# A gated cross-attention block with experts: the attention's gate and sum, and the experts' shares, change places

## The reference

```python
x = x + tanh(g_xattn) * xattn(layernorm(x), ctx, ctx)       # 16 heads of 16, softmax over 512 keys
x = x + tanh(g_ffn) * ffn(layernorm(x))

def xattn(q, k, v):                       # per head
    return softmax(q @ k.T * 16 ** -0.5) @ v

def ffn(x):
    h = x + attention(rmsnorm(x, g1), wq, wk, wv, wo)       # causal, rotary, 16 heads
    return h + moe(rmsnorm(h, g2))

def moe(x):                               # 8 experts, 2 per row
    probs = softmax(x @ w_router)
    topw, topi = top_k(probs, 2); topw = topw / sum(topw)
    return sum_k topw[k] * ((silu(x @ wg[e_k]) * (x @ wu[e_k])) @ wd[e_k])
```

## Time and profile before

| | us |
|---|---|
| median of 3 runs | 1544.46 |
| the runs | 1543.71 to 1545.99 |
| the profiled execution | 1545.92 |
| its span, first to last instruction | 1544.1 |
| TensorE busy | 1426.3 (92%) |
| VectorE busy | 1006.0 (65%) |
| ScalarE busy | 779.5 (50%) |
| GpSimd busy | 881.0 (57%) |
| granted TensorE clock, mean | 0.984 |

### The profile page before, as it was taken

How to read it: one execution, slowest core, us unless ns; L and a number is a source line. 1 busy time by engine, 2 the same in 40 slices (tenths; PEclk the granted TensorE clock), 3 DMA queues, 4 the chain that set the end, 5 groups by cost and what they waited for, 6 DMA issues and landing times.

```text
span 1544.1 us, 30418 instructions
## 1 busy us (share of the span) xinstructions
PE 1426.3 (92%) x9013; PEld 856.7 (55%) x9013; DVE 1006.0 (65%) x2351; ACT 779.5 (50%) x1783; POOL 881.0 (57%) x1147
## 2 busy tenths in 40 slices
PE   3999999999999998999999998878899999999997
PEld 1332334444444444444444545457788888888886
DVE  5888767757766765865864755626665656656564
ACT  1576665665665674565666555543233333333332
POOL 7585776974976977787779687445321222222222
PEclk9899999999999998999999999999999999999999
DMA  7756365474574564555473545383354355255220
GB/s 200 193 169 182 97 204 177 147 221 127 176 218 149 169 198 158 174 171 189 141 219 110 175 145 172 130 308 95 64 150 115 79 150 154 43 150 152 39 41 11
DMA packets 116514, 230.12 MB, mean 149 GB/s; under 512 B 20101, under 2 KB 82949, under 8 KB 114310
## 3 DMA queue, kind: packets, MB, share of 16 engines
q1 hardware_dynamic: 81394, 150.29, 31.9%
q0 software_dynamic: 26032, 69.82, 16.5%
q10 hardware_dynamic: 8932, 8.07, 2.0%
HBM read 135.10 MB, written 93.14 MB: 148 GB/s over the span
## 4 chain that ended last, share of the span: by engine, by line
PE 70%; DVE 9%; POOL 9%; issue 5%; ACT 3%; DMA 2%; SPq 1%; another core or an unknown queue 0%; POOLq 0%; DVEq 0%; ACTq 0%
PE pv_ps L1124 10%; PE max_ps L1086 9%; PE max_ps L779 9%; PE key_ps L779 9%; PE key_ps L1103 8%; PE pv_ps L813 6%; DVE neg L1409 4%; PE aux L1172 3%; PE aux L1163 3%; PE pv_ps L815 3%; PE turn_ps L800 2%; PE aux L1156 2%; ACT probs L1295 2%; POOL w_parts L1751 1%; PE key_ps L1106 1%
## 5 line engine op out<-in xcount | busy, mean ns | idle before, releaser
L1409 DVE TENSOR_REDUCE neg<-max_ps 128x1 f32<-128x512 f32 (+3 forms) x864 | 542.3, 665 | 275.3 <-PE max_ps L1089 173.4
L1295 ACT ACTIVATE probs<-key_ps 128x512 f32<-128x512 f32 (+3 forms) x1024 | 499.3, 519 | 370.2 <-PE key_ps L1106 172.5
L1086 PE MATMUL max_ps<-k_stack,q_stack 96*128 96x512 bf16 (+3 forms) x1024 | 354.7, 350 | 32.8 <-DVE neg L1409 18.8
L1103 PE MATMUL key_ps<-q_stack,k_stack 99*128 99x512 bf16 (+3 forms) x1024 | 349.9, 343 | 21.9 <-ACT probs L1295 14.3
L612 POOL DMA_INDIRECT out<-part,whose x71 | 109.8, 1546 | 349.6 <-DVE part L664 277.0
L1086 PEld LDWEIGHTS max_ps<-k_stack,q_stack 96*128 96x128 bf16 x1024 | 100.8, 99 | 222.3 <-DVE neg L1409 124.7
L1103 PEld LDWEIGHTS key_ps<-q_stack,k_stack 99*128 99x128 bf16 x1024 | 100.6, 98 | 120.5 <-ACT probs L1295 56.6
L813 PE MATMUL pv_ps<-weights,hidden_t 128*128 (+1 forms) x426 | 160.0, 413 | 1.4 <-DVE hidden_t L689 1.4
L779 PE MATMUL max_ps<-weights,rows_t 128*128 (+2 forms) x642 | 154.1, 385 | 0.0
L779 PE MATMUL key_ps<-weights,rows_t 128*128 (+2 forms) x636 | 151.1, 382 | 1.1 <-issue 1.1
L1124 PE MATMUL pv_ps<-probs,v_cross 128*32 128x512 f32 (+3 forms) x1024 | 132.1, 587 | 3.4 <-ACT out_t L1365 2.1
(11 more groups left out here) (240 smaller groups left out, 2237.4 us busy)
## 6 DMA issues: line engine op xcount, KB each, us to landing
w_split<-w_parts POOLq DMA_DIRECT2D x32, 704.0 KB, 5.4
weights<-w_split SPq DMA_DIRECT2D x8, 2816.0 KB
weights<-w_split SPq DMA_DIRECT2D x8, 1280.0 KB
w_split<-w_parts POOLq DMA_DIRECT2D x16, 512.0 KB, 4.1
kept_sb<-kept SPq DMA_DIRECT2D x16, 512.0 KB
rows<-rows_in ACTq DMA_DIRECT2D x61, 129.0 KB
parts_cross_k<-parts_k SPq DMA_DIRECT2D x48, 128.0 KB
parts_cross_q<-parts_q SPq DMA_DIRECT2D x48, 128.0 KB
```

Source lines behind the costliest of these rows:

```text
L1086: r = mm(ps[:, 0:keys], q_stack[g][0:KROWS, hd, qt * P:(qt + 1) * P], k_stack[g][0:KROWS, hd, 0:keys], start=True, stop=not own)
L1103: r = mm(ps[:, q0:S], k_stack[g][0:KROWS + NEGROWS, hd, kt * P:(kt + 1) * P], q_stack[g][0:KROWS + NEGROWS, hd, q0:S], start=True, stop=no ...
L1295: act.activation(probs[:, kt % 2, hd, q0:S], key_ps[j % 2][:, q0:S], ACT.Exp).then_inc(m["exp_done"], 1)
L1409: v.tensor_reduce(neg[:, g % 2, hd - place_:hd + 1, qt], scores, op=ALU.max, axis=AX.X, negate=True).then_inc(m["max_red"], many)
```

## The change

The gate tanh(g_xattn) is multiplied into the values (not into their column of ones), so that the attention comes out gated. The sum of x1 is then a plain add; for batches 2 to 6 GpSimd makes it, first thing in stage 7 of step b - 2, and VectorE only waits for each half before its bn_stats. The first half's unit on VectorE moves from 118 to 122 (and its bn_stats from 119 to 123). For batches 0 to 5 GpSimd makes the shares too, in stage 7 of step b + 1, behind the x1 sum; the reciprocal is a power of -1 there. `values(0)` needs the gate and goes behind `x_rows(1)`.

```diff
-X1_SUMS = {b: at(b - 2, 118, 128) for b in BATCHES} | {0: at(-1, 112, 114), 1: at(0, 46, 48), LAST: at(LAST - 2, 112, 114)}
+X1_SUMS = {b: at(b - 2, 122, 128) for b in BATCHES} | {0: at(-1, 112, 114), 1: at(0, 46, 48), LAST: at(LAST - 2, 112, 114)}
...
+X1_SUM_STAGE = {b: stage(b - 2, 7) for b in range(2, LAST)}
+ROUTE_STAGE = {b: stage(b + 1, 7) for b in range(LAST - 1)}
...
                         act.wait_ge(m["gap_r"], b + 1)
+                        over(act, m["route"], b)
                         act.activation(e_gap[:, :], gap[:, :], ACT.Exp).then_inc(m["gap_exp"], 1)
...
-                v.memset(half[:, :], -0.5)
+                v.memset(half[:, 0:QT], -0.5)
+                v.memset(half[:, QT:2 * QT], -1.0)
...
-                        chain.link(v.tensor_copy(pos_i[:, b % 2, :], pos_f[:, :]))
-                    if c == 2:
+                        v.tensor_copy(pos_i[:, b % 2, :], pos_f[:, :]).then_inc(m["placed"], 1)
+                        dve.wait_ge(m["placed"], b + 1)
+                    if c == 2 and b not in ROUTE_STAGE:
+                        dve.wait_ge(m["route"], b)
                         dve.wait_ge(m["gap_exp"], b + 1)
...
-                        if b == LAST - 2:
-                            put_in_order()
+                    if c == 2 and b == LAST - 2:
+                        dve.wait_ge(m["gap_exp"], b + 1)
+                        put_in_order()
...
-                            chain.link(v.scalar_tensor_tensor(out=x1[:, two, :], in0=att["cross"][:, two, :], scalar=gate[:, 0:1],
-                                                              in1=x1[:, two, :], op0=ALU.mult, op1=ALU.add))
+                            if b in X1_SUM_STAGE:
+                                dve.wait_ge(m["x1_sum"], DC * sorted(X1_SUM_STAGE).index(b) + c + 1)
+                            else:
+                                chain.link(v.tensor_tensor(x1[:, two, :], att["cross"][:, two, :], x1[:, two, :], ALU.add))
...
                     values_read(pool, "cross", b)
+                    pool.wait_ge(m["gate_act"], 1)
                     pool.wait_ge(m["ctx_ld"], (b + 1) * 16)
...
-                                     ctx_in[:, :, :].rearrange("p t (h d) -> p (t h) d", d=DH), 1.0, 0.0, ALU.mult, ALU.add)\
+                                     ctx_in[:, :, :].rearrange("p t (h d) -> p (t h) d", d=DH), gate[:, 0:1], 0.0, ALU.mult, ALU.add)\
...
+                def route(b):
+                    pool.wait_ge(m["gap_exp"], b + 1)
+                    pool.wait_ge(m["h_norm"], b + 1)
+                    chain.link(g_.tensor_scalar(mix[:, 1, :], e_gap[:, :], 1.0, 1.0, ALU.mult, ALU.add))
+                    chain.link(g_.tensor_tensor(mix[:, 0, :], mix[:, 1, :], half[:, QT:2 * QT], ALU.pow))
+                    chain.link(g_.tensor_tensor(mix[:, 1, :], mix[:, 0, :], e_gap[:, :], ALU.mult))
+                    g_.tensor_copy(hn2[b % 2][:, :, D:D + 1], token[:, :].rearrange("p (t e) -> p t e", e=1))
+                    chain.link(g_.tensor_scalar(weight[:, b % 2, :, :].rearrange("p a b -> p (a b)"),
+                                                mix[:, :, :].rearrange("p a b -> p (a b)"), gate[:, 1:2], 0.0, ALU.mult, ALU.add))
+                    g_.tensor_scalar(token[:, :], token[:, :], 1.0, float(S), ALU.mult, ALU.add).then_inc(m["route"], 1)
+
+                def x1_sum(b):
+                    pool.wait_ge(m["xa_ld"], (b + 1) * 16)
+                    pool.wait_ge(m["post_norm"], UNIT_OF["cross", b] * G + 4)
+                    for c in range(DC):
+                        two = slice(2 * c, 2 * c + 2)
+                        g_.tensor_tensor(x1[:, two, :], att["cross"][:, two, :], x1[:, two, :], ALU.add).then_inc(m["x1_sum"], 1)
...
                     pool.wait_ge(m["route"], b + 1)
+                    pool.wait_ge(m["placed"], b + 1)
...
+                        for b, _ in due(X1_SUM_STAGE, now):
+                            x1_sum(b)
+                        for b, _ in due(ROUTE_STAGE, now):
+                            route(b)
                         for b, k in due(ROTATE_STAGES, now):
                             rotate(b, k)
...
-                values(0)
                 x_rows(1)
+                values(0)
```

More of the change, by code:

```diff
@@ L421, in flamingo_block @@
                 x_ld ctx_ld xa_ld kept_ld kept_st base_st x_stat x_rstd x_norm v_cross aux_full aux_free
-                x1_stat x1_rstd x1_norm dve pool xn_done
+                x1_sum x1_stat x1_rstd x1_norm dve pool xn_done
                 rope_cos rope_used x_parts c_parts oq_parts ok_parts x_st0 x_st1 c_st0 c_st1 oq_st0 oq_st1 ok_st0 ok_st1
                 h_sq h_rstd h_norm h_base gap_r gap_exp hot_r
-                rank_r route scat tab_ld pad_at pad first table hn2_twice""".split()
+                rank_r placed route scat tab_ld pad_at pad first table hn2_twice""".split()
             m = {n: sem("s_" + n, st) for n in names}
@@ L1902, in _ @@
                 split("k", "c", flat_k, 0, 1)
+                x_rows(1)
                 values(0)
-                x_rows(1)
                 pool.wait_ge(m["ld_w"], 16 * 5)
```

## The result

The changed kernel takes **1553.92 us** (median of 20 runs, 1548.54 to 1561.84) where the kernel before takes 1544.49 (20 runs): a ratio of 1.0061 (1.005 to 1.0072), 9.4 us slower. The forecast was 1545.9, with 1540.5 to 1551 as its range. The profiled execution took 1552.04 us, its span is 1550.2. Measured twice more, on two different chips, the ratio was 1.0064 (1.0042 to 1.0087) and 1.0022 (1.0006 to 1.0037): the loss is there each time, but its size is 3 to 10 us.

A forecast was written before the change was run, and what follows sets the result against it. VectorE was taken to bound the kernel at step ends, TensorE (92% busy) waiting for it. Terms -0.7 + 0.3 - 1.0 + 2.7 + 0.1 = +1.4 us on the median 1544.46 gave 1545.9 us, range 1540.5 to 1551.

The forecast's parts named there:

- VectorE is saturated at the end of a step: From 493.81 in step 2 VectorE has no idle time for over 10 us, so time removed there counts while TensorE waits.
- The shares and the second sum: VectorE, step ends: shares 1.01 us and unit 128's sum 0.78 go, bn_stats pair adds 0.77; step 1 gains 1.0.
- Step 1's wait for xn: ScalarE's wait in step 1 grows because step 0's moved bn_stats start GpSimd's chain 0.34 us later; +0.3 us.
- step 5: GpSimd's shares ahead of the last batch's x1 rows bring xn at 874.0; between 0 and +0.2 us, taken as 0.1.
- GpSimd's shares are hidden: 2.5 us of shares on GpSimd in steps 2 to 4 end at 502.2, before the split's wait for VectorE ends.
- The start: Moving values(0) behind x_rows(1) shortens VectorE's first subtraction from 1.41 to 0.69 us; -0.7 us, bounds -0.7 to 0.
- The wait: At unit 122 of steps 2 to 4 VectorE waits 1.9 us for GpSimd's first half of x1; bounds 0.5 to 2.3.
- Step 2 did not stand for step 1 to the hundredth: The prediction read step 2's rows for steps 1 to 4, saying these repeat it almost to the hundredth.
- the sum had +0.9: Net of added wait (+1.9) and savings (-1.02) in each of steps 2 to 4; +2.7 us, all terms together +1.4.
- The forecast, with no fall of the clock: The main case: 1545.9 us, TensorE's clock staying 1.00 after unit 122; chance 0.45.
- the rival at 0.27: TensorE's clock falls in the new stall, about 1.7 us each; falls in steps 2 to 4 give 1551; chance 0.27.
- The waits are spread over six maxima: Argument against a clock fall behind unit 122: TensorE's added idle time would be split over six maxima.

The follow-up runs named there:

- the new start: Kernel before with only the first context's values moved on GpSimd behind the first rows of x; +1.1 us (-1.1 to 3.2) against the kernel before.
- the two with a stall: Kernel before with unread maxima added on VectorE at unit 122 of steps 2 to 4: three (+6.3 us, 3.7 to 8.8) or one (+6.3, 4.2 to 8.3).
- the two kernels that kept TensorE busy: Changed kernel, run twice, with the maxima's product made nine times at unit 124 of steps 2 to 4; +6.5 and +4.8 us against the kernel before.
- the long stall: Kernel before plus three unread maxima (2.12 us a step) on VectorE at unit 122 of steps 2 to 4; +6.3 us (3.7 to 8.8).
- the third time: Changed kernel unaltered, measured again on another chip; +3.4 us (0.9 to 5.7) against the kernel before, ratio 1.0022.
- the sums back on VectorE: Changed kernel with VectorE making the x1 sums at 118 and 128, shares still on GpSimd; -3.2 us, again -0.5, against the kernel before.
- the last version: Changed kernel with GpSimd making only the sum's second half, first half on VectorE, statistics at 118 and 128; -2.0 us (-5.1 to 0.9) against before.
- the sums early with statistics at 118: Changed kernel with GpSimd's sums in stage 6 ahead of the scatter, VectorE's statistics at 118 and 128; +0.5 us (-2.9 to 3.7) against before.
- the sums behind the scatter: Changed kernel with GpSimd's sums in stage 6, behind the scatter and ahead of the last weight piece; +0.9 us (-1.5 to 3.6) against before.
- The short stall: Kernel before plus one unread maximum (0.7 us) on VectorE at unit 122 of steps 2 to 4; +6.3 us (4.2 to 8.3).
- the first experiment: Changed kernel with GpSimd's sums moved to stage 6, behind the splitting of the maxima, ahead of the scatter; +1.9 us (-0.6 to 4.5) against before.

## Why the prediction was wrong

**Right.** VectorE is saturated at the end of a step. The shares and the second sum are worth what their rows gave (step 1: -1.06, forecast -1.0; stage 0: -0.79). The wait falls in steps 2, 3 and 4 only. Step 1's wait for xn costs 0.4 (forecast 0.3), step 5 nothing, and GpSimd's shares are hidden.

**The start** was taken at its gaining end. The subtraction did become 0.7 us shorter, but the load of the queries goes out at 24.03 instead of 23.89 us. Unit 0 starts at 28.59 to 28.90 in the four profiles with the old order and at 28.31 to 28.64 in the fourteen with the new one: the term is -0.3, not -0.7. By itself the new order measured +1.1 us (-1.1 to +3.2).

**The wait** was sized 1.9 us and is 2.55. VectorE reaches unit 122 0.37 us sooner after the stage's start than forecast (9.78 against 10.15), and it goes on 0.26 us later, 1.64 us after the adds began where 1.27 + 0.1 were allowed. The 10.15 was not VectorE's own pace: in steps 2 to 4 of the trace of before a gap beside the indirect DMAs lets the reduction behind VectorE's idle time start 7.38 us into stage 7, 0.57 us after the end of its product where step 1 has 0.14. In step 1, and in steps 2 and 3 of three other profiles with the work of the kernel before (the one with the new start, and the two with a stall), it starts at 6.94 or 6.95, and VectorE comes to unit 122 at 9.70 to 9.72. Step 2 did not stand for step 1 to the hundredth, and the rows of step 1 would have shown it. VectorE's rows of step 1, whose stage 7 starts at 365.65:

```profile
372.60 0.69 DVE L1409 TENSOR_REDUCE neg<-max_ps 128x2 f32<-128x512 f32 x1 [0.73 <-PE max_ps L1089]
...
375.36 0.16 DVE L1505 TENSOR_SCALAR mix<-e_gap 128x4 f32<-128x4 f32 x1
```

A step's stages 7 and 0 come to +1.95 - 0.79 = +1.2 us where the sum had +0.9, and the ten stages to +2.2 us: as a count of stages against that one trace the sum, +1.4, was nearly right. But 0.44 us in each of the three steps is the gap of that trace. On a chip without gaps the kernel before has about 13.71 us there and not 14.15, so an estimate from these stage lengths is +2.2 + 3 x 0.44 = +3.5 us.

**The step that failed** is the choice of "The forecast, with no fall of the clock", against the rival at 0.27. The clock fell behind the wait in all three steps of the first profile, for 6.8 us each, in two of three in the second, in all three in the third; never behind it in the two kernels that kept TensorE busy, and never at this place in those with neither the wait nor the long stall. "The waits are spread over six maxima" was the argument against it, and it was wrong: TensorE's wait is one stretch of 2.17 us. The size given, 1.7 us a fall, held for the three falls of the first profile (1.73, 2.24, 1.73); on the mean of the eight falls in three profiles it is 1.2 us. Even that rival's 1551 would have been short, by the wait and the start that were mis-sized and by what follows.

**What stays open.** By that estimate 3.5 us of stages, 0.4 us of ScalarE's wait in step 1 and 2 to 6 us of half clock behind the waits make 6 to 10 us, against +9.4 and +9.9 measured where the profiles show no gaps; on the chip of the third time, whose profiles have gaps, 2.2 + 0.4 + 2.3 make 4.9, against +3.4 (0.9 to 5.7). The parts fit, but no run prices each by itself.

For the other versions the stages alone do not give the time: nearly every one lies 1 to 8 us above them. The record holds a large part of the reason. The mean granted clock is below that of the kernel before in every comparison, the harmless ones too. Within one kernel on one chip, over the 291 runs here that have a clock on record, a run with 0.01 less of mean clock takes 7.9 us more (5 to 7 in the kernel before alone); the price of the falls above gives the same, since 0.01 of 1550 us is 31 us at half clock, and 6.8 us of it cost 1.7. With this taken out, the sums back on VectorE come to -5.2 and -4.2 us (stages: -5.4), the last version to -4.3 (-8.2), the sums early with statistics at 118 to -2.7 (-5.1), the sums behind the scatter to -2.5 (-5.6): estimates, but all gains. The short stall stays unexplained, +5.1 against +1.5. Why the clock is granted lower elsewhere in the kernel when these stages are altered was not found.

## What to carry to other kernels

An engine that works in order takes new work only behind what it has; ask where its queue stands when the result is wanted, and hand over the half that is wanted late. A wait that stops TensorE in one piece for 2 us should be priced with a fall of its clock as the likely case: here it came behind 8 of 9. Before one step stands for the others, lay its rows beside theirs. And a gain of 5 us counted in stages is no gain until the runs show it: here four such versions measured between -3 and +1, with a lower clock each time.

## What the runs showed of the hardware

**What TensorE makes reaches the other engines late beside indirect DMAs, in some profiles.** The gaps of the first experiment come to 8 to 15 us a profile in all twelve profiles taken on three of the chips and in that of the kernel before, single ones up to 2.7 us, and to exactly none in the first profile of the changed kernel and in all four profiles taken on a fourth chip, with the same indirect DMAs of 1.0 us each. The ends of matmuls are modelled in these records, so they do not show whether TensorE itself stands still; what causes the gaps was not found. It means that stage lengths of profiles from different chips differ by up to 2.2 us where nothing was changed: stages 3 and 5 of step 6 (14.65 and 13.91 us before, 13.04 and 11.74 after) are such, and no part of the result. Stages 7 of steps 2 to 4 of the trace of before are such too, by 0.44 us.

**VectorE can be held for the whole of GpSimd's adds.** In the kernel with the shares back on VectorE, its product of two tiles of 128x4 in SBUF took 3.07 us instead of 0.16 in step 3, and in step 2 an operation with one such tile (`tensor_scalar`, 128x4) took 3.14. The reductions from PSUM beside such adds keep their 0.56 us, and the bn_stats, which read x1 in SBUF, their 0.74. The Trainium skill (SBUF — State Buffer, "Who interferes with whom") has the port pair that the two share as a lock, kept for the whole instruction: whichever starts second stands until the first is done. Here VectorE's record starts 0.4 us ahead of the adds and yet ends with them, and stands through both.
